# Cross-attention: the query packing transfers move from SP's queue to ScalarE's

## The reference

```python
x = x + xattn(layernorm(x), ctx_1024, mask, Wq, bq, Wk, bk, Wv, bv, Wo, bo)
# inside xattn, 16 heads of 16 features:
q = split_heads(hidden @ Wq.T + bq)        # 32 x 16 x 100 x 16
k = split_heads(ctx @ Wk.T + bk)           # 32 x 16 x 361 x 16
v = split_heads(ctx @ Wv.T + bv)
scores = where(mask == 0, -inf, q @ k.T / 4)
out = softmax(scores) @ v
return merge_heads(out) @ Wo.T + bo
```

## Time and profile before

| | |
|---|---|
| time, median of 3 runs | 2025.49 us (2003.54 to 2041.23) |
| time of the profiled execution | 2018.95 us |
| its span | 2017.2 us |
| PE busy | 1678.1 us, 83% |
| DVE, ACT, POOL busy | 1049.7, 771.3, 535.2 us |
| PE's mean granted clock | 0.845 of full speed |
| SP's query packing | 384 transfers, 591 ns median to issue |
| SP's key packing | 384 transfers, 590 ns median to issue |
| cross-attention, first to last score tile | 868.6 to 1584.5 us of the span |

### The profile page before, as it was taken

One profiled execution on the slowest core, in us unless ns is written; L12 is line 12 of the kernel. 1 busy time (PEld: TensorE's weight loads), 2 busy tenths in 40 slices (PEclk: granted clock), 3 DMA queues, 4 the chain that ended last, 5 costly groups with the idle time before them and its releaser, 6 DMA issues. The chain is left out here.

```text
span 2017.2 us, 39918 instructions
## 1 busy us (share of the span) xinstructions
PE 1678.1 (83%) x12244; PEld 1462.5 (73%) x12244; DVE 1049.7 (52%) x2565; ACT 771.3 (38%) x1832; POOL 535.2 (27%) x753
## 2 busy tenths in 40 slices
PE   2999999999999999467788788887888750999998
PEld 2788888887888888456676667666777650788887
DVE  4756565656647464244555555455555330555553
ACT  3545454545535353123444444444444310222221
POOL 1102020102020201333334333333333206333332
PEclk9887979799969696668888888889888655899999
DMA  7302020202020202143343333334333205355542
GB/s 238 81 1 66 1 65 0 65 0 65 6 59 10 55 17 50 41 110 87 90 101 87 96 94 94 91 91 98 96 92 79 70 0 159 107 189 171 189 164 89
DMA packets 151229, 164.63 MB, mean 82 GB/s; under 512 B 70908, under 2 KB 127779, under 8 KB 150916
## 3 DMA queue, kind: packets, MB, share of 16 engines
q1 hardware_dynamic: 144324, 152.92, 28.4%
q0 software_dynamic: 3968, 6.59, 1.0%
q10 hardware_dynamic: 2880, 4.40, 0.7%
HBM read 83.39 MB, written 26.95 MB: 55 GB/s over the span
## 5 line engine op out<-in xcount | busy, mean ns | idle before, releaser
L1127 DVE TENSOR_REDUCE row_max<-psb_s 100x1 f32<-100x361 f32 x512 | 263.3, 529 | 241.7 <-PE psb_s L1264 237.4
L1264 PE MATMUL psb_s<-k,q 97*100 97x362 f32 x512 | 206.5, 406 | 140.5 <-DMA k<-k_st 95.2
L1028 ACT ACTIVATE probs<-psb_t 121x400 f32<-121x400 f32 (+1 forms) x384 | 193.5, 505 | 184.8 <-PE psb_t L1274 178.8
L381 POOL TENSOR_TENSOR diag<-neg_ident,row_max 100x400 fp32r<-100x400 f32 x128 | 106.6, 854 | 464.4 <-PE ps_t L614 320.8
L1264 PEld LDWEIGHTS psb_s<-k,q 97*100 97x100 f32 x512 | 98.2, 192 | 167.7 <-issue 95.1
L1274 PE MATMUL psb_t<-q,k 98*121 98x200 f32 (+1 forms) x768 | 167.2, 304 | 1.3 <-ACT probs L1028 1.3
L1274 PEld LDWEIGHTS psb_t<-q,k 98*121 98x121 f32 (+1 forms) x768 | 147.1, 211 | 5.1 <-ACT probs L1028 1.9
L1943 PE MATMUL psd_h<-h_in,w_sb 128*128 128x256 f32 x640 | 144.5, 385 | 1.4 <-ACT h_in L1809 1.4
L1951 PE MATMUL psd_y<-w_sb,hid 128*128 128x256 f32 x640 | 144.5, 379 | 0.0
L1943 PEld LDWEIGHTS psd_h<-h_in,w_sb 128*128 128x128 f32 x640 | 123.7, 193 | 19.1 <-issue 1.8
L1951 PEld LDWEIGHTS psd_y<-w_sb,hid 128*128 128x128 f32 x640 | 120.1, 190 | 15.5
(11 more groups left out here) (228 smaller groups left out, 4043.2 us busy)
## 6 DMA issues: line engine op xcount, KB each, us to landing
w_sb<-in_w SPq DMA_DIRECT2D x40, 1024.0 KB, 7.4
k<-k_st SPq DMA_DIRECT2D x384, 90.5 KB
q<-q_st SPq DMA_DIRECT2D x384, 50.0 KB
v_rows<-v_tok SPq DMA_DIRECT2D x32, 400.0 KB
v_ext<-v_rows SPq DMA_DIRECT2D x32, 400.0 KB
c_t<-in_contextT SPq DMA_DIRECT2D x32, 361.0 KB, 3.1
routed_rows<-empty SPq DMA_DIRECT2D x1, 5140.0 KB, 20.7
rows<-routed_rows SPq DMA_DIRECT2D x20, 257.0 KB, 8.2
```

The lines of the kernel that those rows point to most:

```text
L381: pool.tensor_tensor(diag[:, g % 2], c.neg_ident[0:S, 0:S].unsqueeze(1).to_broadcast([S, GH, S]), row_max[:, g // 2 % 2, g % 2].unsqueeze( ...
L1028: act.activation(probs[0:KT[kt], u % 2, kt], ps_t[i % 2][0:KT[kt], 0:4 * S], ACT.Exp, scale=HD2 ** -0.5).then_inc(probs_ready, 1)
L1127: dve.reduce_max(row_max[:, p, h:h + 1], ps_s[h % 2][0:S, 0:S2], AX_X).then_inc(max_ready, 1)
L1264: pe.matmul(ps_s[h % 2][0:S, 0:S2E], q2[0:97, p, u, g, S * a:S * (a + 1)], k2[0:97, p, u, g], start=True, stop=True).then_inc(scores_ready, 1)
```

## The change

The six query transfers leave `pack` and become a function `pack_queries` in ACT's list. ACT calls it for the first half right behind `exps(b, 2, 2)` and for the second half right behind `exps(b, 3, 2)`, the last group of the step. The bias and the keys stay on SP, which no longer waits for `q_lo_ready`. What PE waits for, 13 transfers on each `packed` semaphore, is as before. Ahead of the loop, the calls for batches 0 and 1 stand behind `x_turned(1, 1)` and `queries(1, 1)`.

```diff
             def pack(b, p, half):
                 ready = packed[p][half]
                 reach(sp, shifted_ready, (b - 2) * 12 + (6 * half + 6))
-                sp.wait_ge(q_lo_ready, b + 1)
-                for u in (2 * half, 2 * half + 1):
-                    rows = slice(32 * u, 32 * u + 32)
-                    for at, part in ((0, 0), (32, 0), (64, 1)):
-                        sp.dma_start(q2[at:at + 32, p, u].bitcast(F32),
-                                     q_st[rows, p, part].rearrange("p g a s -> p g (a s)").bitcast(F32)).then_inc(ready, 16)
                 bias = kb_dram[row(b), :]
...
+            def pack_queries(b, p, half):
+                reach(act, shifted_ready, (b - 2) * 12 + (6 * half + 6))
+                act.wait_ge(q_lo_ready, b + 1)
+                for u in (2 * half, 2 * half + 1):
+                    rows = slice(32 * u, 32 * u + 32)
+                    for at, part in ((0, 0), (32, 0), (64, 1)):
+                        act.dma_start(q2[at:at + 32, p, u].bitcast(F32),
+                                      q_st[rows, p, part].rearrange("p g a s -> p g (a s)").bitcast(F32)
+                                      ).then_inc(packed[p][half], 16)
...
             x_turned(1, 1)
+            pack_queries(0, 0, 0)
+            pack_queries(0, 0, 1)
             keys(1, 1, 0)
             keys(1, 1, 1)
             queries(1, 1)
+            pack_queries(1, 1, 0)
+            pack_queries(1, 1, 1)
...
                 exps(b, 2, 2)
+                if more(b, 2):
+                    pack_queries(b + 2, p, 0)
                 if not (isinstance(b, int) and b == 0):
                     turned_out(b - 1)
...
                 exps(b, 3, 2)
+                if more(b, 2):
+                    pack_queries(b + 2, p, 1)
```

## The result

The changed kernel takes 2051.61 us (median of 4 runs, 2045.69 to 2055.01), the kernel before 2017.26 us beside it (2003.54 to 2041.23). The ratio is 1.019, with a 95% interval of 1.011 to 1.027: slower, clear of the scatter of the runs, and just under the 2% that I had named as the limit.

What follows compares the result with a forecast made beforehand. Bound: the cross-attention chain h0, queries, POOL, SP, next h0, with keys queued behind queries. Three kinds of step, +0.46, +1.23 and +0.05 us, summed to +17 us on 2018.95: 2036 us, range 1995 to 2080.

Steps and rivals of the forecast that it cites:

- block 1: ACT's six first-half query issues ahead of `turned_out`: 3.95 us, delaying PE's `project` by 1.72, 0.22 or 1.27 us a step.
- block 2: ACT's six second-half issues ahead of the next `exps(0,0)`: next `shifted(0,2)` no earlier than about 4.6 us after `exps(3,2)`.
- the clock: PE's granted clock in the cross-attention, low after some waits: mix of fast and slow steps assumed as before, no cost added.
- What bounds the kernel before: Cross-attention chain h0, queries, POOL, SP, next h0 sets the period; PE waits 94.3 us for keys queued behind queries.
- The transfers off SP cost nothing and the wait at h0 goes: SP loses six issues per half, 3.70 us; PE's key wait at score tile h0 goes; ACT's first-half queries arrive just in time.
- the lower bound: ACT's issue might start while the ACTIVATE ahead still runs: up to 0.5 us less per block, -15 to -25 us in all.
- the first part: Part of a step from `shifted(0,2)` to the end of `exps(2,2)`; forecast to change by 0.
- rival 2: Clock falls in every step after the roughly 3 us wait: 2062 to some 2085 us, stage clock near 0.8; chance 0.27.
- the third: Part of a step from `project` to the end of `exps(3,2)`; forecast to change by 0.
- Rival 1: SP's and ACT's queues hold each other up: block 2 takes about 3.7 us more, about 2145 us; chance 0.06.
- Rival 3: ACT's issue slips under the ACTIVATE, or the clock falls less often: 1985 to 2020 us; chance 0.19.
- Rival 4: ACT's issues cost PE nothing and the whole wait goes: 94.3 us less, 1925 us; chance 0.04.

Runs made afterwards that it cites:

- experiment 1: Kernel before, all transfers kept on SP, but in each half bias and keys issued first and the six queries last; 1870.71 us, ratio 0.9245.
- experiment 4: Changed kernel plus ten score-tile-sized matmuls on PE ahead of `shifted(0,2)` in each step, their result overwritten; 1992.55 us, ratio 0.9841 to the kernel before.
- experiment 5: Kernel before plus ten score-tile-sized matmuls on PE ahead of h0 in each step, their result overwritten; 1983.75 us, ratio 0.9853.
- experiment 2: Changed kernel with only the first half's queries issued by ACT, the second half's back on SP ahead of its keys; 1913.02 us, ratio 0.9531 to the kernel before.
- experiment 6: Changed kernel with all twelve query issues on ACT, but two at a time behind six ACT operations; 1949.08 us, ratio 0.9656 to the kernel before.

## Why the prediction was right, and where it was not

*The result.* 2051.6 us lies in the range of 1995 to 2080, 16 above the 2036 on record, and on the side that I forecast. The change of the stage was +17 by the sum and is +37 us. That the time still lies in the range is in part luck: block 1 came out 20 us cheaper than its term (30 x 0.67), block 2 4 us dearer, and the clock, which had no term, took 31 to 35 us.

*What bounds the kernel before.* Right as a chain: experiment 1 cut the link of keys behind queries and the wait was gone. That the wait also carried a second cost, the slow matmuls behind it, I had seen but not counted. The wait was 94 us, and its removal without a price on ACT gave a stage 134 us shorter.

*The transfers off SP cost nothing and the wait at h0 goes.* Right. No row of the changed profile has PE waiting for a transfer, and ACT's first group was in time.

*Block 2.* "That one can't start before ... about 4.6 us after the end of `exps(3,2)`": 4.61 on average. The picture of an old and a new wait at nearly the same place held: PE waits 2.5 us at `shifted(0,2)` in place of 2.0 or 3.6 at h0.

*Block 1.* I had 4.6 us to `project`; it is 4.03. The issues start with the ACTIVATE ahead of them, so 0.5 us of the block is hidden. This is what I had named as the lower bound and had not taken. At block 2 0.4 us is hidden in the same way, and it went into the slower issue beside SP (0.25) and the longer way to the next ACTIVATE (0.28 us in the median and up to 0.62, against 0.11).

*The clock: the step that failed.* "I let the mix be as before." The mix did not stay. Before, from the fifth step on, the first part had no low stretch behind any wait of about 2.0 us, and had one behind each of 3.5 to 3.8. The new wait, 2.5 to 2.9 us in every step, has one behind it in every step, and it ends so that nearly all of the stretch lies on work: 5.3 us of the first part in place of 2.6. This is rival 2, to which I gave 0.27; but the sign that I set for it, a clock of the stage near 0.8, did not come (0.86), because the mean does not show where the low time falls. It gave +1.03 us in the first part and the greater part of the +0.13 in the third, where the forecast had none: 31 to 35 of the 37 us. Experiments 4 and 5 show it in both kernels by filling only the wait. The two errors, block 1 too dear and the clock at nothing, partly cancelled.

*Rival 1, the two queues.* 0.25 us a block, not 3.7: six issues of ACT and six of SP side by side take 4.04 and 3.82 us, alone 3.79 and 3.73. In experiment 2, six of SP beside the first issues of block 1 took 4.1 in the median. The Trainium skill, Perfetto Trace Analysis, "DMA Instruction — HWDGE (DVE, Sync)", says that a DMA instruction locks the shared descriptor generator for exclusive use, and that the wait for the lock counts in its time. The trace agrees that there is some delay, but not that the two queues take turns issue by issue. Whether the lock is its cause no run here shows.

*Rival 3.* Its first half, the issue that slips under the ACTIVATE, happened. Alone it would have made the kernel a little faster than forecast.

*Rival 4, issues that cost nothing on ACT.* Not at these two places. With the twelve issues spread (experiment 6) ACT carries them at 3.4% less than before, and one group alone (experiment 2) at 4.7% less.

*What stays open.* Why no low stretch follows a wait of 2.04 us at h0, while one follows a wait of 2.50 us at `shifted(0,2)` and in experiment 2 in one step of three even two waits of about 1 us, and why one step in four of the changed kernel loses less than the others: the runs show the outcomes and not the rule. Nor did I take apart why the first part of a step is 11.4 us in experiment 1 and 10.8 in experiment 4, both at the high level there.

## What to carry to other kernels

Before a transfer is moved to a queue that has other work, look at the order in the queue that it is in: here the ready keys stood behind the unready queries, and exchanging them gave 7.5%, where the second queue gave -1.9%. If issues have to go on an engine with an ordered list, put no more of them in a row than the lead of the engine that waits for it. And count a wait of PE twice where the clock falls after it: once for itself, and once for the matmuls behind it that run at half the clock. Where that stretch falls matters as much as the length of the wait.

## What the runs showed of the hardware

- ACT's queue starts to issue a transfer when the ACTIVATE ahead of it starts: 1042.20 and 1042.20, 1048.17 and 1048.26. Over the stage it is 0.00 us later at block 1 and 0.09 at block 2 (medians). The next ACTIVATE then comes 0.11 us after the last issue behind block 1, and 0.15 to 0.62 behind block 2.
- An issue of 32 partitions takes ACT 0.63 us and SP 0.62 us (3.79 and 3.73 for six); six of them beside the other queue's six take 0.25 and 0.09 us more.
- Ten extra matmuls of 0.17 us in a wait of 2 to 3.6 us took 20.6 us off the stage before and 44 off the changed one. The granted clock of the stage rose from 0.87 to 0.94 and from 0.86 to 0.91.
- With the waits mostly gone it was 1.00 over 450 us at a PE that is busy 90% of the time (experiment 1), as here between 950 and 1400:

```profile
950.00:1400.00 450.00, 407.23 (x4669) 346.57 (x4668) 291.31 (x621) 243.62 (x621) 198.09 (x298) 1.00 0.47 116
```
